# Attention output of a fused AdaLN block on Trainium2: the other operand stationary, in column strips

## The reference

```python
logits = jnp.einsum('bhqd,bhkd->bhqk', q, k) * d ** (-0.5)
attn = jax.nn.softmax(logits, axis=-1)
o = jnp.einsum('bhqk,bhkd->bhqd', attn, v)
o = jnp.swapaxes(o, 1, 2).reshape(b, n, dim)
return o + o @ W_out
```

## Time and profile before

| | us |
|---|---|
| runs of the kernel (median of 3; lowest, highest) | 1108.74 (1106.15, 1109.91) |
| profiled execution, its time | 1109.38 |
| its span, first to last instruction | 1107.5 |
| TensorE busy | 1060.1 |
| VectorE busy | 854.9 |
| ScalarE busy | 804.6 |
| GpSimd busy | 553.8 |
| mean granted TensorE clock, share of full speed | 0.98 |

### The profile page before, as it was taken

How to read it: one execution, slowest core, us unless ns; L and a number is a source line. 1 busy time by engine, 2 the same in 40 slices (tenths; PEclk the granted TensorE clock), 3 DMA queues, 4 the chain that set the end, 5 groups by cost and what they waited for, 6 DMA issues and landing times.

```text
span 1107.5 us, 24385 instructions
## 1 busy us (share of the span) xinstructions
PE 1060.1 (96%) x9457; PEld 668.5 (60%) x9457; DVE 854.9 (77%) x1614; ACT 804.6 (73%) x1370; POOL 553.8 (50%) x365
## 2 busy tenths in 40 slices
PE   8568899999999999999999999999999999999898
PEld 2234565656666665766666576666656666665665
DVE  4877768787877968788796878878687877877656
ACT  4767686868778685877868586786858687684954
POOL 1832290835638092653819274471917447281613
PEclk9769899999999999999999999999999999999999
DMA  9910303131121313122131312213131311212100
GB/s 339 342 32 15 88 20 78 63 77 59 29 74 44 95 46 78 58 40 63 44 96 44 78 59 52 65 31 94 44 77 59 66 56 37 46 39 58 58 20 20
DMA packets 79521, 77.12 MB, mean 70 GB/s; under 512 B 8624, under 2 KB 59952, under 8 KB 78896
## 3 DMA queue, kind: packets, MB, share of 16 engines
q1 hardware_dynamic: 79408, 75.58, 24.5%
HBM read 41.85 MB, written 8.40 MB: 45 GB/s over the span
## 4 chain that ended last, share of the span: by engine, by line
PE 90%; DVE 4%; ACT 3%; issue 1%; POOL 1%; DMA 1%; SPq 0%; ACTq 0%; DVEq 0%
PE F L950 10%; PE F L951 10%; PE F L783 10%; PE F L785 10%; PE QA L714 4%; PE QA L715 4%; PE QA L716 4%; PE QB L714 3%; PE QB L715 3%; PE QB L716 3%; PE T L996 3%; PE SB L842 2%; PE SA L842 2%; PE PV L859 2%; PE PV L858 2%; PE PV L857 2%
## 5 line engine op out<-in xcount | busy, mean ns | idle before, releaser
L950 PE MATMUL F<-yT_hi,fc_t 128*128 128x256 f16 x1024 | 228.2, 274 | 0.0
L951 PE MATMUL F<-yT_lo,fc_t 128*128 128x256 f16 x1024 | 227.8, 274 | 0.0
L664 POOL TENSOR_TENSOR rqk<-ssq,half 128x16 f32<-128x16 f32 x64 | 194.1, 3038 | 45.7 <-DVE ssq L1476 45.7
L783 PE MATMUL F<-proj_t,hs 128*128 128x512 f16 x512 | 194.6, 380 | 0.0
L785 PE MATMUL F<-proj_t,hs 128*128 128x512 f16 x512 | 194.2, 379 | 0.0
L633 POOL TENSOR_TENSOR acc<-acc,hg 128x512 f32<-128x512 f32 x96 | 150.0, 1562 | 15.7 <-ACT hg L1111 2.8
L1437 DVE SCALAR_TENSOR_TENSOR hs<-hg,g_inv,hs 128x512 f16<-128x512 f32 x128 | 104.8, 819 | 64.8 <-ACT hs L1116 64.7
L633 POOL TENSOR_TENSOR acc<-hg 128x512 f32<-128x512 f32 x16 | 20.3, 1269 | 211.0 <-ACT hg L1111 183.3
L1111 ACT ACTIVATE hg<-F,g_fc 128x512 f32<-128x512 f32 x128 | 87.3, 682 | 46.2 <-PE F L951 46.1
L640 POOL TENSOR_TENSOR acc<-acc,hq 128x512 f32<-128x512 f32 x90 | 114.1, 1267 | 13.4 <-ACT hq L1184 4.8
L627 POOL TENSOR_TENSOR rs<-var,half 128x1 f32<-128x1 f32 x32 | 17.6, 551 | 203.4 <-DVE var L1305 203.4
(11 more groups left out here) (227 smaller groups left out, 2727.0 us busy)
## 6 DMA issues: line engine op xcount, KB each, us to landing
stk<-qkT SPq DMA_DIRECT2D x128, 128.0 KB, 2.4
xtok<-in_x SPq DMA_DIRECT2D x17, 512.0 KB, 3.9
xT_sb<-in_xT SPq DMA_DIRECT2D x16, 512.0 KB, 3.5
stk<-qkT SPq DMA_DIRECT2D x128, 64.0 KB, 2.1
xres<-in_x SPq DMA_DIRECT2D x15, 512.0 KB, 3.6
out<-xres SPq DMA_DIRECT2D x15, 512.0 KB, 2.8
stk<-in_w_emb SPq DMA_DIRECT2D x4, 512.0 KB, 6.9
fc_t<-in_w_qkv SPq DMA_DIRECT2D x2, 1024.0 KB, 11.4
```

What stands on the lines that cost most here:

```text
L664: pool.tensor_tensor(rqk[:, n % 2, :], ssq[:, n % 2, :], half[:, :], ALU.pow).then_inc(rqk_r, 1)
L783: pe.matmul(FB[t][:, :], hs[:, 0, k // 2, col:col + P], proj_t[:, k, :], start=(k == 0), stop=False)
L950: pe.matmul(dst, w, yT_hi[:, k, :], start=(k == 0), stop=False)
L951: mm = pe.matmul(dst, w, yT_lo[:, k, :], start=False, stop=(k == KT - 1))
```

## The change

The product is turned round. v is stationary, 32 columns for a head, and p moves with 256 columns. Head j of a group of four has its v in columns 32j to 32j+31 of the array and its output in the same partitions of bank PV, so the result of a group is 128 (head, feature) by 256 (queries), which is already the form of oT. For each half of the keys, four heads are issued one behind the other for v_hi with p_hi, v_lo with p_hi, v_hi with p_lo: 24 matmuls in a group. The row sums come from a 128x32 tile of ones as the stationary operand, with p_hi and p_lo moving: 16 more, into columns 256 to 511 of PV, every sum repeated over 32 partitions. The reciprocal is then taken of 128x256 elements. No transposes of the output follow; oT_hi and oT_lo are made from o_sb, which now has one buffer, released by a new semaphore `olo_r`.

`values` runs by group, at heads 5, 9, 13 and at the end. heads_out stands at 6, 10 and 14 on VectorE, heads_hi at the same heads on ScalarE, heads_lo at 7, 11 and 15. p has eight slots; xn1 shares the memory of the upper four of p_lo. At the end of the iteration ScalarE has v_hi, v_hi, oT_hi(3) and VectorE the residual, v_lo, v_lo, heads_out(3), heads_lo(3).

```diff
-BEHIND = 2
+SLOTS = 2 * HPG
-END = [HEADS - 2] + V[1][1:2] + [HEADS - 1] + V[1][2:4]
+END = V[1][1:4]
+VALUES_AT = {5: 0, 9: 1, 13: 2}
+HEADS_OUT_AT, HEADS_HI_AT, HEADS_LO_AT = {6: 0, 10: 1, 14: 2}, {6: 0, 10: 1, 14: 2}, {7: 0, 11: 1, 15: 2}
-TURN_AT = {4: ("piece", 0), 6: ("heads", 0), 7: ("piece", 1), 8: ("rms", 0), 10: ("heads", 1),
-           11: ("piece", 2), 12: ("stats", 0), 13: ("piece", 3), 15: ("heads", 2)}
+TURN_AT = {4: ("piece", 0), 7: ("piece", 1), 8: ("rms", 0), 11: ("piece", 2), 12: ("stats", 0), 13: ("piece", 3)}
...
-        rden = sb("rden", [P, TT, HPG])
-        o_sb = sb("o_sb", [P, 2, TT, P])
+        rden = sb("rden", [P, N])
+        o_sb = sb("o_sb", [P, N])
...
+        def wait_slot(engine, att, h):
+            if h >= SLOTS:
+                engine.wait_ge(pv_done, nth(att, GROUPS, (h - SLOTS) // HPG + 1))
+            elif live(att - 1):
+                engine.wait_ge(pv_done, nth(att - 1, GROUPS, (h + HEADS - SLOTS) // HPG + 1))
...
-                def values(h):
-                    g, j = h // HPG, h % HPG
-                    pe.wait_ge(plo_r, nth(att, HEADS, h + 1))
...
-                    for t in range(TT):
-                        dst = PV[:, (t * HPG + j) * VW:(t * HPG + j + 1) * VW]
-                        for k in range(TT):
-                            ph = p_hi[:, h % (BEHIND + 1), k, t * P:(t + 1) * P]
-                            pe.matmul(dst, ph, v_hi[:, k, h, :], start=(k == 0), stop=False)
-                            pe.matmul(dst[:, 0:DH], ph, v_lo[:, k, h, :], start=False, stop=False)
-                            mm = pe.matmul(dst, p_lo[:, h % (BEHIND + 1), k, t * P:(t + 1) * P], v_hi[:, k, h, :],
-                                           start=False, stop=(k == TT - 1))
+                def values(g):
+                    def add(cols, weights, moving, first=False, last=False):
+                        for j in range(HPG):
+                            mm = pe.matmul(PV[DH * j:DH * j + DH, cols], weights(HPG * g + j), moving(HPG * g + j),
+                                           start=first, stop=last)
+                        return mm
...
+                    if g > 0 or live(att - 1):
+                        pe.wait_ge(o_r, nth(att, GROUPS, g) if g else nth(att - 1, GROUPS, GROUPS))
+                    pe.wait_ge(plo_r, nth(att, HEADS, HPG * (g + 1)))
+                    out, total = slice(0, N), slice(N, 2 * N)
+                    for k in range(TT):
+                        add(out, lambda h: v_hi[:, k, h, :], lambda h: p_hi[:, h % SLOTS, k, :], first=(k == 0))
+                        add(out, lambda h: v_lo[:, k, h, :], lambda h: p_hi[:, h % SLOTS, k, :])
+                        add(out, lambda h: v_hi[:, k, h, :], lambda h: p_lo[:, h % SLOTS, k, :], last=(k == TT - 1))
+                    for k in range(TT):
+                        add(total, lambda h: ones16[:, 0:DH], lambda h: p_hi[:, h % SLOTS, k, :], first=(k == 0))
+                        mm = add(total, lambda h: ones16[:, 0:DH], lambda h: p_lo[:, h % SLOTS, k, :],
+                                 last=(k == TT - 1))
                     mm.then_inc(pv_done, 1)
-                def heads_turn(g):
-                    pe.wait_ge(o_r, nth(att, GROUPS, g + 1))
-                    open_turn(("heads", g))
-                    for t in range(TT):
-                        mm = pe.transpose(T[:, t * P:(t + 1) * P], o_sb[:, g % 2, t, :], ident[:, :])
-                    mm.then_inc(turned, 1)
...
-                    pe.wait_ge(unturned, turn_base(i) - 1)
+                    pe.wait_ge(olo_r, nth(ffn, GROUPS, KT - 1))
...
                 if att is not None:
-                    heads_turn(GROUPS - 1)
+                    values(GROUPS - 1)
...
                 if qkv is not None and not first(qkv):
                     value_hi(qkv, 0)
-                if att is not None:
-                    heads_hi(i, att, GROUPS - 1)
                 if qkv is not None and not first(qkv):
                     value_hi(qkv, 1)
+                if att is not None:
+                    heads_hi(att, GROUPS - 1)
...
             def heads_out(att, g):
-                dve.wait_ge(pv_done, nth(att, HEADS, HPG * (g + 1)))
-                pv = PV[:, 0:TT * HPG * VW].rearrange("p (t j w) -> p t j w", t=TT, j=HPG)
+                dve.wait_ge(pv_done, nth(att, GROUPS, g + 1))
                 if g or live(att - 1):
-                    dve.wait_ge(o_r, nth(att, GROUPS, g) if g else nth(att - 1, GROUPS, GROUPS))
-                dve.reciprocal(rden[:, :, :], pv[:, :, :, DH]).then_inc(rden_r, 1)
+                    dve.wait_ge(olo_r, nth(att, GROUPS, g) if g else nth(att - 1, GROUPS, GROUPS))
+                dve.reciprocal(rden[:, :], PV[:, N:2 * N]).then_inc(rden_r, 1)
                 dve.wait_ge(rden_r, nth(att, GROUPS, g + 1))
-                dve.tensor_tensor(o_sb[:, g % 2, :, :].rearrange("p t (j d) -> p t j d", j=HPG), pv[:, :, :, 0:DH],
-                                  rden[:, :, :].unsqueeze(3).to_broadcast([P, TT, HPG, DH]), ALU.mult
-                                  ).then_inc(o_r, 1)
+                dve.tensor_tensor(o_sb[:, :], PV[:, 0:N], rden[:, :], ALU.mult).then_inc(o_r, 1)
...
-                if att is not None:
-                    heads_out(att, GROUPS - 1)
                 if ffn is not None:
                     residual(ffn, 1)
                 if qkv is not None and not first(qkv):
                     value_lo(qkv, 0)
+                    value_lo(qkv, 1)
                 if att is not None:
+                    heads_out(att, GROUPS - 1)
                     heads_lo(att, GROUPS - 1)
-                if qkv is not None and not first(qkv):
-                    value_lo(qkv, 1)
```

More of the change, by code:

```diff
@@ L191, in turn_uses @@
     _, ffn, att, qkv, pre = stages(i)
-    runs = {"y": ffn, "stats": ffn, "max": att, "heads": att, "piece": qkv, "rms": pre}
+    runs = {"y": ffn, "stats": ffn, "max": att, "piece": qkv, "rms": pre}
     if pre is not None and not early(pre):
         runs["rms"] = None
-    uses = [("y", 0), ("y", 1), ("max", 0)] + [turn_at(i)[slot] for slot in sorted(turn_at(i))] + [("heads", 3)]
+    uses = [("y", 0), ("y", 1), ("max", 0)] + [turn_at(i)[slot] for slot in sorted(turn_at(i))]
     return [use for use in uses if runs[use[0]] is not None]
@@ L279, in adaln_ffn_kernel @@
         stk = sb("stk", [P, HEADS, 2, N], F16)
-        v_hi = sb("v_hi", [P, TT, HEADS, VW], F16)
+        v_hi = sb("v_hi", [P, TT, HEADS, DH], F16)
         v_lo = sb("v_lo", [P, TT, HEADS, DH], F16)
@@ L294, in adaln_ffn_kernel @@
         nb1 = sb("nb1", [P, TT])
-        xn1 = sb("xn1", [P, TT, D])
+        xn1 = p_lo[:, HPG:SLOTS, :, :].rearrange("p s k n -> p (s k n)").bitcast(F32).rearrange("p (t d) -> p t d", t=TT)
         yT_hi = sb("yT_hi", [P, KT, N], F16)
@@ L984, in iteration @@
                         between(item)
-                    if att is not None and h >= BEHIND:
-                        values(h - BEHIND)
+                    if att is not None and h in VALUES_AT:
+                        values(VALUES_AT[h])
                     if last(att) and h >= HEADS - 2:
+                        pe.wait_ge(plo_r, nth(att, HEADS, HEADS - 3))
                         keep_busy(SB[0], h - HEADS + 3)
@@ L1004, in iteration @@
                         mm.then_inc(turned, 1)
-                    if kind == "heads" and att is not None:
-                        heads_turn(n)
                     if kind == "stats" and ffn is not None:
@@ L1015, in iteration @@
                 for item in END:
-                    if isinstance(item, tuple):
-                        if not first(qkv):
-                            between(item)
-                    elif att is not None:
-                        values(item)
+                    if not first(qkv):
+                        between(item)
                 if last(att):
@@ L1167, in iteration @@
                                        ACT.Identity, scale=g_k[:, 0:1] if w else 1.0).then_inc(qkhi_r, 1)
-                    if kind == "heads" and att is not None:
-                        heads_hi(i, att, n)
+                    if att is not None and h in HEADS_HI_AT:
+                        heads_hi(att, HEADS_HI_AT[h])
                     if isinstance(i, int) and i == 0 and h in SIGN_AT:
@@ L1188, in value_hi, with heads_hi @@
                 if live(b - 1):
-                    act.wait_ge(pv_done, nth(b - 1, HEADS, HEADS))
+                    act.wait_ge(pv_done, nth(b - 1, GROUPS, GROUPS))
                 act.activation(v_hi[:, t, :, 0:DH], QB[t][:, :].rearrange("p (h d) -> p h d", h=HEADS),
                                ACT.Copy, scale=V_SCALE / QKV_SCALE).then_inc(vhi_r, 1)
-            def heads_hi(i, att, g):
-                act.wait_ge(turned, turn(i, ("heads", g)) + 1)
+            def heads_hi(att, g):
+                act.wait_ge(o_r, nth(att, GROUPS, g + 1))
                 if live(att - 1) and g == 0:
```

(6 more changed lines are left out.)

38 lines of the change are left out of this document (15 added, 23 removed).

## The result

The changed kernel takes 1259.8 us (median of 4 runs, 1258.9 to 1261.6) against 1107.9 (1106.2 to 1109.9) on the same chip: a ratio of 1.137, 95% interval 1.135 to 1.138. Forecast were 1240 us and a range of 1150 to 1290. The profiled execution took 1259.65 us with a span of 1257.4.

The account below looks back on a forecast made before the run. TensorE, busy 96% of the span, was taken as the bound. 1109.4 us + 107 (14 iterations at +7.7) + 12 (first and last iterations) + 12 (clock falls) = 1240 us, range 1150 to 1290.

Parts of the forecast that it names:

- The walk: Steady iteration followed step by step from the end of values(0): stalls of 8.4 us against 0.7 saved on TensorE.
- reciprocal 128x256: VectorE, heads_out: 1.7 to 2.2 us by the slope per element, taken as 2.0; 7.2 us more per iteration.
- scores(8) and (9): Head loop after heads_out(0): TensorE stalls of 0.8 and 0.2 us, waiting for banks freed by p_lo.
- scores(12), wait: Head loop: heads_out(1) delays p_lo(10), so these scores go at 13.15 instead of 11.0, a stall of 2.15 us.
- values(3), wait: End of head loop: late heads_out(2) holds ScalarE and p_lo(15); start at 26.55 instead of 23.7, a stall of 2.85 us.
- The rival that they take turns: In values: column strips run one after another, 4.6 us a group, 1400 us in all; chance 0.07.
- the shared bank T loses four users: Bank T in the iteration: loses four users, listed among the things unchanged or costing nothing; no stall put there.
- The clock: TensorE's granted clock falls after long stalls, 1.7 us each; one fall in two iterations, 12 us, from nothing to 48.
- this case: The main forecast, slow wide reciprocal stalling TensorE: 1240 us, own range stated as 1195 to 1290; chance 0.73.
- The ends: First and last iterations: 6 us more each, for the four reciprocals' 7.2 us with a little of it covered.
- The reciprocal costs what any other 256 elements cost: At L1325: 0.42 us instead of 0.2, leaving only the iteration's end stall of 0.9; 1112 us; chance 0.13.
- Slack serves better: VectorE queue: some work comes earlier, leaving some 4 us of stalls at scores(12) and the end; 1167 us; chance 0.07.

Follow-up runs that it names:

- e_copy: The changed kernel with the wide reciprocal replaced by a multiplication by 2 to the power of -16, the division left out: 1168.8 us, ratio 1.054.
- e_bnarrow: The kernel before plus one multiplication by a constant on 128x256 elements of PV in heads_out on VectorE: 1120.0 us, ratio 1.011.
- e_bwide: The kernel before plus one 128x256 reciprocal of PV into an unread buffer, in heads_out ahead of the small one: 1202.9 us, ratio 1.085.

## Why the prediction was right, and where it was off

The walk with its zero at the end of values(0) (600.90 in the trace above), forecast and measured:

| step | forecast | measured |
|---|---|---|
| group of strips | 1.3 us | 1.30 |
| reciprocal 128x256 | 2.0 (1.7 to 2.2) | 1.75 |
| scores(8) and (9) late by | 0.8 and 0.2 | 0.26 and 0.23 |
| heads_out(1) begins | 10.0 | 9.6 |
| scores(12), wait | 13.15, 2.15 | 12.44, 1.74 |
| turn of the sums in bank T, wait | none | 15.27, 1.14 |
| heads_out(2) begins | 21.7 | 22.3 |
| values(3), wait | 26.55, 2.85 | 26.98, 2.59 |
| group_max(0), wait | 2.4 | 2.36 |
| an iteration, net | +7.7 | +8.15 |

- **The strips** came out as the row strips of the earlier trace rows said. The rival that they take turns is out. TensorE's saving of some 0.6 us an iteration stands in the rows (16 x 0.30 + 4 x 0.26, less 4 x 1.30), but in no run does it outweigh the waits.
- **The reciprocal** costs 6.2 ns for each element beyond the eighth, (1748 - 206) / 248: the lower of the two slopes from the earlier trace rows. That is also below the 2.2 us which my estimate gave from the page VectorE: DVE Perf Modes of the Trainium skill with its repeat count of 8. I chose 2.0 where the lower slope, from 0.163 to 0.206, gave 1.7.
- **The step that failed** is "the shared bank T loses four users", which I costed at nothing. The bank did lose them, but its next user, the turn of the sums, waits for a q, k low half (615.35) that stands behind heads_out(1), two p_lo, two other wide instructions and heads_lo(1) on VectorE. I followed the score banks through VectorE's queue, and not T. At 1.3 us an iteration it is 17 us. The other waits came out below their forecasts: 0.5 us instead of 1.0 at scores(8) and (9), 1.7 instead of 2.15 at scores(12), 2.6 instead of 2.85 at values(3). The errors cancel, so that +7.7 for +8.15 is partly luck, and better than its parts.
- **The clock** was, beside that term put at nothing, the most mis-sized one. The mechanism was right and so was the price (1.7 forecast, 1.6 measured), but a fall in every second iteration was too few: 15 that cost time in 13 iterations, 23.5 us instead of 12.
- **The range.** The working gives 1211 to 1287 us (1240 less 17 and 12, or plus 11 and 36); the 1195 stated as this case's lower end follows from none of its terms.
- **The ends.** The first iteration, the start and the tail took 20.7 us together, where 12 + 7.7 were set for the same part.
- **The rivals.** "The reciprocal costs what any other 256 elements cost" forecast 1112 us for a product in its place; e_copy has such a product, and took 1169. So that case was wrong beyond its premise: it counted only the end of the iteration and missed values(3) behind p_lo(15) and bank T. "Slack serves better" (1167) didn't occur as the kernel stands.

Beyond the forecast is the second cause. I put the whole loss on the division's length, and 60 of the 152 us remain without it. Four heads in a lump mean that values(3) waits for p_lo(15) with no other attention work left to do, where before only the last head's twelve matmuls were behind it. Of the 60, mending the order recovered 42. That the last 18 are due to the lumps is argued, not shown: no run had strips for fewer than four heads. Another candidate is the wide product that stands in for the division: it takes 0.42 us where before the small reciprocal took 0.21, and in e_bnarrow 0.42 us more at each place cost 11 us. Half of that, an estimate of 6 us from that run, could be its part of the 18. What also stays open is whether an order exists in which the division fits; VectorE has 14.6 us free in an iteration after (72.10 less 57.54), and in each of the orders tried something stood in front of the wrong instruction.

## What to carry to other kernels

Price a rewrite by the narrowest queue it touches: here 0.6 us was saved on TensorE by giving VectorE a division over 128x256 copies of what had been 128x8 numbers, 1.75 us where a product of that size takes 0.42. An engine with a fifth of its time free had no room here, because the work landed in front of the instruction that frees a bank; and every bank that it frees has to be followed, not only those next to the change. Put a price on the granted clock wherever a change makes TensorE wait: the falls were 23.5 of the 152 us here, and e_copy had them with no wait over 1.4 us.

## What was not expected of the hardware

- The reciprocal's price is linear and not in steps: 128x8 0.206 us, 128x128 0.948, 128x256 1.748, so 6.2 ns an element throughout. Right behind the wide reciprocal, the small one of 128x8 took only 0.144 us (median of 64, in e_bwide) instead of 0.206.
- The same waits of 2.6, 2.4, 1.7 and 1.1 us gave no fall of the clock in the iteration from 562.2 us and two in that from 486.95. A fall cost 1.6 us or nothing, by whether a wait followed that could take it up, so the iterations come in steps of 1.6 us (72.1, 73.7, 75.3).
- A logarithm directly followed by an exponential loaded a table for each of the two, 64 times each at 1.28 us.
